# Late stage of a mixture-of-experts kernel: two down-projection rows interleaved, activation sums and combine steps moved among the chunks

## The reference, cut to what matters

```python
x0 = einsum('bct,bcd->bdt', x, weights[subjects])          # xf: 4096 rows of 512
h  = silu(xf @ expert_fc1[e].T) * (xf @ expert_fc2[e].T)   # F = 352
y  = sum over the two chosen experts e of p_e * (h @ expert_proj[e].T)
s  = silu(xf @ shared_fc1.T) * (xf @ shared_fc2.T)         # FS = 1408 = 11 chunks of 128
y += sigmoid(xf @ shared_gate_w.T) * (s @ shared_proj.T)
out = x + y
```

## Time and profile before

| what | us |
|---|---|
| median of three runs | 1300.14 (1299.24 to 1305.26) |
| profiled execution, its own time | 1301.66 |
| its span | 1299.5 |
| PE busy | 1260.2 (97%) |
| DVE busy | 865.5 (67%) |
| ACT busy | 488.9 (38%) |
| POOL busy | 293.1 (23%) |

### The profile page before, as it was taken

How to read it: one execution, slowest core, us unless ns; L and a number is a source line. 1 busy time by engine, 2 the same in 40 slices (tenths; PEclk the granted TensorE clock), 3 DMA queues, 4 the chain that set the end, 5 groups by cost and what they waited for, 6 DMA issues and landing times.

```text
span 1299.5 us, 20327 instructions
## 1 busy us (share of the span) xinstructions
PE 1260.2 (97%) x7006; PEld 1079.0 (83%) x7006; DVE 865.5 (67%) x1410; ACT 488.9 (38%) x821; POOL 293.1 (23%) x431
## 2 busy tenths in 40 slices
PE   6999999999999999999999999999998998998998
PEld 5878888888888999999999999998776776786876
DVE  5544444459645777687778777787677667678675
ACT  4322231121012666566666665554223213213211
POOL 4576671000001212212222121100130131031030
PEclk9999999999999999999999999999999999999999
DMA  9597866201234777767767867675965864864852
GB/s 318 190 322 277 291 212 241 105 33 65 98 125 155 274 258 268 259 239 279 266 225 269 289 224 254 248 270 191 335 205 176 267 195 162 263 217 156 269 158 104
DMA packets 110670, 284.29 MB, mean 219 GB/s; under 512 B 11570, under 2 KB 11698, under 8 KB 104850
## 3 DMA queue, kind: packets, MB, share of 16 engines
q1 hardware_dynamic: 96738, 229.25, 50.0%
q0 software_dynamic: 13872, 54.27, 13.4%
HBM read 217.16 MB, written 66.32 MB: 218 GB/s over the span
## 4 chain that ended last, share of the span: by engine, by line
PE 79%; issue 10%; DVE 5%; DMA 2%; POOL 2%; ACT 1%; POOLq 1%; SPq 0%; DVEq 0%
PE bank_h L864 41%; PE bank_o L864 24%; PE bank_h L1126 4%; PE bank_t L1126 3%; PE bank_t L854 2%; POOL rows L784 2%; PE bank_t L864 1%; DMA xf_transposed<-xt 1%; PE bank_t L811 1%; POOLq L782 1%; PE bank_o L821 1%; ACT h_hi L1177 1%; DVE rawp L1792 1%; DVE raw L1818 0%; DVE raw L1827 0%
## 5 line engine op out<-in xcount | busy, mean ns | idle before, releaser
L864 PE MATMUL bank_h<-x_hi,w_hi 128*128 128x256 f32 (+2 forms) x1096 | 349.5, 319 | 4.4 <-DVE x_lo L1655 2.6
L864 PE MATMUL bank_h<-x_hi,w_lo 128*128 128x256 f32 (+2 forms) x1096 | 343.4, 313 | 0.0
L864 PE MATMUL bank_h<-x_lo,w_hi 128*128 128x256 f32 (+2 forms) x1096 | 342.7, 313 | 0.0
L864 PE MATMUL bank_o<-wp_hi,h_hi 128*128 128x512 f32 (+1 forms) x565 | 234.3, 415 | 23.1 <-DVE res L1839 15.4
L864 PE MATMUL bank_o<-wp_lo,h_hi 128*128 128x512 f32 (+1 forms) x565 | 231.4, 410 | 0.0
L864 PE MATMUL bank_o<-wp_hi,h_lo 128*128 128x512 f32 (+1 forms) x565 | 229.9, 407 | 0.0
L864 PEld LDWEIGHTS bank_h<-x_hi,w_hi 128*128 128x128 f32 (+1 forms) x1096 | 201.0, 183 | 16.8 <-issue 5.5
L864 PEld LDWEIGHTS bank_h<-x_hi,w_lo 128*128 128x128 f32 (+1 forms) x1096 | 201.0, 183 | 12.6
L864 PEld LDWEIGHTS bank_h<-x_lo,w_hi 128*128 128x128 f32 (+1 forms) x1096 | 201.1, 183 | 11.2
L1695 DVE TENSOR_TENSOR w_lo<-raw,w_hi 128x704 fp32r<-128x704 f32 x156 | 132.5, 886 | 55.4 <-ACT w_hi L1177 55.4
L864 PEld LDWEIGHTS bank_o<-wp_hi,h_hi 128*128 128x128 f32 (+1 forms) x565 | 107.9, 191 | 53.5 <-DVE res L1839 20.6
(11 more groups left out here) (222 smaller groups left out, 2023.1 us busy)
## 6 DMA issues: line engine op xcount, KB each, us to landing
raw<-ew SPq DMA_DIRECT2D x39, 1408.0 KB, 7.3
rawp<-ewp SPq DMA_DIRECT2D x39, 512.0 KB, 7.9
w_early<-late_up SPq DMA_DIRECT2D x72, 256.0 KB, 3.7
slot_rows<-res SPq DMA_DIRECT2D x32, 512.0 KB, 4.6
x_hi<-late_up SPq DMA_DIRECT2D x48, 256.0 KB, 3.5
x_lo<-late_up SPq DMA_DIRECT2D x48, 256.0 KB, 4.2
xt_in<-xf_transposed SPq DMA_DIRECT2D x11, 1024.0 KB, 7.5
late_up<-raw POOLq DMA_DIRECT2D x6, 1792.0 KB, 7.7
```

Of the source, the lines that this page charges most:

```text
L864: mm = pe.matmul(dst, a, m, start=(first and i == 0), stop=(last and i == 2))
```

## The change

On PE the rows 0 and 1 of a team are worked together: of chunks 0 and 1 of the team first row 0 and row 1, then of chunk 2 both; rows 2 to 7 as before. On DVE picks 0 and 1 stand before chunks 1 and 2, picks 2 to 5 behind rows 0, 2, 4, 6, and picks 6 and 7 before chunks 3 and 5; sum 0 stands before chunk 3, sums 1 and 2 before chunk 4, sum 3 before chunk 5. Nothing else is moved, and no work is added or taken away.

```diff
+            def late_part(b, g, r, jj):
+                j = g * TEAM + jj
+                if jj == 0:
+                    at_least(pe, late.o_kept, (b * TEAMS + g) * HROWS + r - 1)
+                if r % BT == 0:
+                    pe.wait_ge(late.h_lo, 2 * (b * LATE + j) + r // BT + 1)
                 c = slice(r * P, (r + 1) * P)
+                m = product(bank_o[r % 2][:, :], (late_h[0][:, jj, c], late_h[1][:, jj, c]),
+                            (late_wp(0, j), late_wp(1, j)), jj == 0, jj == TEAM - 1)
+                if jj == TEAM - 1:
+                    m.then_inc(late.o_full, 1)
+
+            def late_rows(b, g):
+                for jj in range(TEAM - 1):
+                    for r in range(2):
+                        late_part(b, g, r, jj)
+                for r in range(2):
+                    late_part(b, g, r, TEAM - 1)
+                for r in range(2, HROWS):
+                    for jj in range(TEAM):
+                        late_part(b, g, r, jj)
...
             for b in range(HBLOCKS):
                 for j in range(TEAM):
-                    late_chunk(b * LATE + j, HROWS * b if j == TEAM - 1 else None)
+                    if j:
+                        late_pick(HROWS * b + j - 1)
+                    late_chunk(b * LATE + j)
                 for r in range(HROWS):
                     late_row(b, 0, r)
                     if r % 2 == 0:
-                        dve.wait_ge(late.o_kept, b * TEAMS * HROWS + r + 1)
-                        late_pick(HROWS * b + 1 + r // 2)
+                        at_least(dve, late.o_kept, b * TEAMS * HROWS + min(r, 2 + r // 2) + 1)
+                        late_pick(HROWS * b + 2 + r // 2)
                 for j in range(TEAM):
-                    late_chunk(b * LATE + TEAM + j, HROWS * b + HROWS - TEAM + j)
+                    if j != 1:
+                        late_pick(HROWS * b + 6 + j // 2)
                     if b + 1 < HBLOCKS:
-                        late_sum(b + 1, j)
-                if b + 1 < HBLOCKS:
-                    late_sum(b + 1, 3)
+                        for q in ((0,), (1, 2), (3,))[j]:
+                            late_sum(b + 1, q)
+                    late_chunk(b * LATE + TEAM + j)
```

More of the change, by code:

```diff
@@ L1149, in late_chunk @@
                 late_product(n, P3, bank_c, False)
-            def late_row(b, g, r):
-                at_least(pe, late.o_kept, (b * TEAMS + g) * HROWS + r - 1)
-                c = slice(r * P, (r + 1) * P)
[L1155 to L1161, removed]
+            def late_part(b, g, r, jj):
[4 more added lines that the diff above has]
+                    pe.wait_ge(late.h_lo, 2 * (b * LATE + j) + r // BT + 1)
+                c = slice(r * P, (r + 1) * P)
+                m = product(bank_o[r % 2][:, :], (late_h[0][:, jj, c], late_h[1][:, jj, c]),
[11 more added lines that the diff above has]
+                        late_part(b, g, r, jj)
             for b in range(HBLOCKS):
@@ L1170, in _ @@
                             pe.wait_ge(ex.o_kept, 2 * XT)
-                    for r in range(HROWS):
-                        late_row(b, g, r)
+                    late_rows(b, g)
         @block.scalar
@@ L1798, in late_c12, with late_chunk @@
                 nc.vector.tensor_tensor(g2_sb, bank_h[1][:, :], u2_sb, ALU.add).then_inc(late.c12, 1)
-            def late_chunk(n, pick=None):
+            def late_chunk(n):
                 jj, at = n % TEAM, PRODUCTS * n + 1
@@ L1811, in late_chunk @@
                 nc.vector.tensor_tensor(h2_sb, bank_h[1][:, :], u3_sb, ALU.add).then_inc(late.c22, 1)
-                if pick is not None:
-                    late_pick(pick)
                 dve.wait_ge(late.p_full, at + P4)
```

## The result

The changed kernel takes 1309.35 us (median of 6 runs, 1307.11 to 1311.86) against 1301.6 (median of 6) for the kernel before, measured beside it (1299.24 to 1305.26). The ratio is 1.0059, 95% interval 1.004 to 1.0079: slower by 0.6%. The profiled execution has a span of 1306.0 us (before 1299.5), 6.5 us more, and its own time is 1308.09.

What follows compares the result with a forecast made beforehand. PE was busy 1260.2 of 1299.5 us, with team 1 of blocks 0 to 2 bound by DVE from pick 5's landing. Costs of 3.6 + 4.8 + 0.5 = 8.9 us on the median 1300.14 gave 1309, range 1301 to 1314.

Steps and rivals of the forecast that it cites:

- The new stall in chunk 3: PE waits before P3 of chunk 3 for c22, 5.0 us after the third landing; 6.2 us in block 1.
- The landing stays: The third landing of gathered data behind the rows, now pick 6's, stays at 1057.70 in block 1.
- Landing to row 2: In blocks 0 to 2, row 2 behind team 1 begins 33.1 us after the third landing, before 30.3.
- The clock: PE's clock falls behind the chunk 3 stall, costing 1.6 us, and no longer at row 2 behind team 1.
- Blocks 0 to 2: Team 1 of these blocks: a cost of 1.2 us each, 3.6 in all.
- Block 3: No sums to win from; 3.2 us of PE stall and 1.6 for the clock, a cost of 4.8 us.
- Picks 0 and 1 early: Ahead of chunks 1 and 2: cost 0, but 0.5 us taken in block 0, from 0 to 1.5 allowed.
- The interleaving: Rows 0 and 1 on PE: 0 us, eight times; the rival, 0.08, had it win about 7 us, 1302.
- the gathers in time: Rival, 0.12: pick 6's data is there when DVE is through with row 7; 12 us won, 1288.
- the kept clock: Rival, 0.12: the clock does not fall at chunk 3; row 2 at third landing (L) + 31.7, 1303.
- the gathers that slip further: Rival, 0.08: block 0's early gathers meet full DMA queues, later landings move 2 us or more a block; 1315 and over.
- The quick gather of the Trainium skill: Rule weighed, not used: 2.6 us per 256 KB gather DMA, making block 1's chunk 3 stall about 1 us.

Runs made afterwards that it cites:

- e4: The changed kernel with pick 6 alone put back inside chunk 3, behind c22; 1288.7 us, ratio 0.9907 to the kernel before.
- e5: The changed kernel with idle matmuls added on PE in chunk 3 of blocks 0 to 3, before the wait for c22; 1303.55 us, ratio 1.0032.
- e1: The kernel before with the interleaving of rows 0 and 1 on PE alone, DVE untouched; 1302.37 us, ratio 0.9999.
- e9: The changed kernel with PE's rows in the old order; 1308.56 us, ratio 1.0067.
- e7: The changed kernel with its picks placed anew and DVE emptying rows 0 and 1 inside a team's last chunk; 1283.53 us, ratio 0.9875.
- e8: The same as e7, but with PE's rows in the old order; 1286.05 us, ratio 0.9889.
- e10: e7 with picks behind rows 0, 2 and 6, the one left over inside chunk 3 (block 0: chunks 3 and 4); 1277.49 us, ratio 0.9826.

## Why the prediction was right, point by point

1309 was forecast and 1309.35 measured, and the mechanism is the one forecast: the stall at chunk 3 costs more than the sums taken from row 2 win. That the number fits to 0.35 us is partly luck. The difference that was added is 8.9 us, and 7.8 was measured by the medians (7.4 in the late stage of the profiled pair); the baseline measured beside the changed kernel is 1.5 us higher than the one added to. And in blocks 0 to 2 three errors of up to 2 us cancel in part, as the points below show.

- **The new stall in chunk 3.** c22 reaches PE 5.05 us after the third landing in blocks 0 to 2, as summed. Stalls were forecast at 6.2 in block 1 and 3.2 in block 3, and the waits read 5.53 and 3.15. e4 took it away and the loss with it.
- **The landing stays.** 1057.70 before and 1057.79 after in block 1. Measured from row 2 behind team 0 it came 1.2 us earlier in block 1 (21.5 for 22.7) and 1.1 in block 2, and a little later in blocks 0 and 3. That is the largest miss of the sum: I had held these waits for unchanged. The first gather behind the rows of block 1 is issued 1.13 us after its index copy (1037.83 to 1038.96), where it took 1.97 before; in block 2 that step differs by 0.2 only. The cause was not tried.
- **Landing to row 2.** 33.1 forecast, and 33.6, 33.8 and 33.2 measured, against 30.3 before. The 0.1 to 0.7 too little is the price of the clock behind the stall. P3 and chunk 4 up to its P3 were summed at 11.2 us with 1.6 for the clock, and took 11.7, 11.9, 11.3 and 11.2 us in blocks 0 to 3 (a product's 1.36 less than the 13.09, 13.28, 12.64 and 12.53 from the first matmul of P3 to that of chunk 5). Without 9.52 and 0.1 that is a price of 2.1 and 2.3 us behind the waits of 4.50 and 5.53, and of 1.7 and 1.6 behind those of 3.79 and 3.15. It shows on DVE as a wait of c21 for P4 of 0.9 to 1.1 us in blocks 0 and 1, and c12 follows the last products as summed.
- **The clock.** It stays at 1.00 behind the new row 2, which gives back 1.6 to 2.0 us a block (1.6 in the sum), and falls behind the stall in all four blocks (0.56, 0.53, 0.72 and 0.72 over the six microseconds from 960, 1062, 1163 and 1262); e5 shows that it costs time. The drop at 3.15 us of idle in block 3 was a choice between rows of 1.03 and 3.43, and held. In the late stages of all thirteen traces the clock fell behind every wait of 2.86 us and more. Of the waits from 1.78 to 2.79 it fell behind some (1.78, 1.92, 2.64) and stayed at 1.00 behind others (1.99, 2.44, 2.79). The kernel before has one of them, which the choice left out: a wait of 1.78 us in the rows of block 0 (945.54), with the clock at 0.72 behind it.
- **Blocks 0 to 2.** Forecast +1.2 each, measured +1.9, +0.3 and +0.1: 2.3 for 3.6 in all. No block shows the 1.2 that was given to each. Against the sum, the landings take off 2.0 us over the three blocks and the clock behind row 2 another 0.6, and the dearer drop behind the stall adds 1.3.
- **Block 3.** Forecast +4.8; 26.98 us from landing to row 2 before and 31.78 after is +4.8.
- **Picks 0 and 1 early.** 0 in blocks 1 to 3; in block 0 pick 0 waits 1.38 us for its data and PE 0.65 before P3 of chunk 1, and the stretch up to row 2 is 0.1 longer (0.5 allowed).
- **The interleaving.** Forecast 0, and e1 (0.9999) and e9 (1.0067 against 1.0059) show it. That rival, at 0.08, is out; so are the gathers in time (the third still ends a wait of 4.2 to 5.0 us) and the kept clock, and the gathers that slip further: none landed more than 0.3 us later behind row 2 of team 0. The kept clock's L + 31.7 should have been L + 31.5 by the terms of the sum (33.1 less 1.6), which leaves its 1303 as it is; e5 measured 31.8 to 31.9.
- **The quick gather of the Trainium skill.** By the estimate of 2.6 us a DMA from its page DMA: Bandwidth & Descriptors (Anatomy of one DMA — SWDGE (gpsimd) path) the stall would have been about 1 us in block 1. The trace does not agree: it was 5.53.

## What to carry to other kernels

A step that waits for a transfer must not stand ahead of instructions that another engine waits for: one such step a block, put ahead of three short instructions and a sum, cost this kernel 20 us (1.0059 against 0.9907). When a change moves several things, sum each against the same fixed event (here the landing of one gather), since a large gain and a larger loss can make a small number. And an order on one engine that is worth nothing while another's chain sets the pace may be tried again once that chain is shortened; e7 and e8 do not settle whether it is worth something then.

## What the runs showed that was not expected

The waits in the rows and those in the chunks are coupled through the gathers. In e7 row 0 of team 0 was emptied 1.4 us earlier, and most of that came back as a wait of 1.16 us before row 7, until the picks were spread (e10, 6.8 us by the two medians). The lower clock also costs time in a chain that PE does not bound, 1.4 to 2.0 us a block in e5, since one DVE instruction waits for the slow product. And the drop is not of one price: it cost 1.6 us behind a wait of 3.15 and 2.3 behind one of 5.53.
